# Hybrid window/banded attention with top-2 experts on one core: one rolling queue of rows per expert, expert outputs added straight into the output by accumulating transfers, and VectorE's evictions of them at the end of a step

## What is computed

```
x = x + window_attention(group_norm(x))     # 8x8 windows, shifted by 4, 8 heads, cosine scores, relative bias
t = t + banded_attention(layer_norm(t))     # blocks of 128 tokens, 4 heads, causal band of 32
t = t + experts(layer_norm(t))              # 8 experts, the 2 likeliest of each token, 128 -> 256 -> 128, exact gelu
    probs = softmax(xf @ gate_w + gate_b);  top2_vals, top2_idx = top_k(probs, 2)
    acc = acc + cw[:, e, None] * (gelu(xf @ W1[e] + b1[e]) @ W2[e] + b2[e])
```

## Time and profile before

| | us |
|---|---|
| median of 3 runs (2977.64 to 3004.55) | 2999.1 |
| the profiled execution | 2989.77 |
| its span, first to last instruction | 2988.0 |

### The profile page before, as it was taken

One profiled execution on the slowest core, in us unless ns is written; L12 is line 12 of the kernel. 1 busy time (PEld: TensorE's weight loads), 2 busy tenths in 40 slices (PEclk: granted clock), 3 DMA queues, 4 the chain that ended last, 5 costly groups with the idle time before them and its releaser, 6 DMA issues. The chain is left out here.

```text
span 2988.0 us, 75732 instructions
## 1 busy us (share of the span) xinstructions
PE 2511.1 (84%) x27338; PEld 1770.3 (59%) x27338; DVE 1996.7 (67%) x5193; ACT 1872.4 (63%) x3478; POOL 1670.3 (56%) x1626
## 2 busy tenths in 40 slices
PE   6888898888998889889989898888988787766673
PEld 3465555656666666666666666665666565544452
DVE  3678877887666666776766687777866676543223
ACT  3666666667667677677777677777766565443231
POOL 1224445554333444565555566777637888877765
PEclk9999999999999999899999899999999798977897
DMA  6233344335445554153443444554433333347674
GB/s 216 103 115 124 132 166 158 128 129 201 135 135 177 171 182 166 59 155 101 123 123 112 119 135 117 149 148 131 137 105 111 113 107 98 100 129 256 193 240 158
DMA packets 255504, 422.65 MB, mean 141 GB/s; under 512 B 42044, under 2 KB 141512, under 8 KB 252688
## 3 DMA queue, kind: packets, MB, share of 16 engines
q1 hardware_dynamic: 209632, 322.59, 33.5%
q0 software_dynamic: 35456, 72.95, 8.1%
q10 hardware_dynamic: 10048, 22.28, 2.4%
HBM read 205.05 MB, written 231.63 MB: 146 GB/s over the span
## 5 line engine op out<-in xcount | busy, mean ns | idle before, releaser
L1308 POOL DMA_INDIRECT x_sorted<-xn_c,place_i x512 | 537.1, 1049 | 333.5 <-PE bank_s L780 127.4
L1298 POOL TENSOR_TENSOR s_sb_a<-s_sb_a,mx_a 128x512 f32<-128x512 f32 x256 | 268.0, 1047 | 675.9 <-DVE mx_a L1703 675.0
L1329 POOL DMA_INDIRECT yg<-y_sorted,place_i x320 | 317.7, 993 | 187.9 <-PE bank_to L863 84.1
L1695 DVE TENSOR_TENSOR s_sb_a<-bank_s,bias_a 128x512 f32<-128x512 f32 x256 | 176.5, 690 | 327.1 <-PE bank_s L780 242.7
L1320 POOL DMA_INDIRECT y_tokens<-yo,back_to x276 | 284.9, 1032 | 93.8 <-issue 73.9
L909 PE MATMUL bank_m<-xe,wk_e 128*128 128x512 f32 x552 | 279.5, 632 | 47.6 <-ACT hid L1176 27.9
L917 PE MATMUL bank_m<-wk_e,hid 128*128 128x128 f32 x2208 | 288.0, 294 | 1.2 <-ACT hid L1176 1.2
L917 PEld LDWEIGHTS bank_m<-wk_e,hid 128*128 128x128 f32 x2208 | 282.5, 211 | 2.6 <-issue 1.9
L1298 POOL TENSOR_TENSOR s_sb_b<-s_sb_b,mx_b 128x512 f32<-128x512 f32 x256 | 269.9, 1054 | 0.3
L1142 ACT ACTIVATE p_sb_a<-s_sb_a 128x512 f32<-128x512 f32 x256 | 160.8, 628 | 161.0 <-POOL s_sb_a L1298 160.5
L841 PE MATMUL bank_to<-k_consts,p_sb_b 128*128 128x128 f32 x1024 | 178.5, 300 | 91.3 <-ACT pt_sb_a L1137 66.0
(11 more groups left out here) (233 smaller groups left out, 5947.0 us busy)
## 6 DMA issues: line engine op xcount, KB each, us to landing
y_sorted<-t_back SPq DMA_DIRECT2D x192, 512.0 KB, 5.2
wk_e<-in_w_experts_dram SPq DMA_DIRECT2D x134, 321.0 KB
xs<-x_sorted SPq DMA_DIRECT2D x134, 258.0 KB
y_sorted<-yo SPq DMA_DIRECT2D x101, 256.0 KB
t_kept<-t SPq DMA_DIRECT2D x64, 256.0 KB
xin<-in_x_dram SPq DMA_DIRECT2D x128, 112.0 KB
x_res<-in_x_dram SPq DMA_DIRECT2D x256, 56.0 KB
t_back<-t_kept SPq DMA_DIRECT2D x23, 512.0 KB
```

Source lines behind the costliest of these rows:

```text
L1298: pool.tensor_tensor(s[:, :, :], s[:, :, :], m[:, :, None].to_broadcast(shape), ALU.subtract).then_inc(s_sub[w], 1)
L1308: pool.indirect_dma_start(out=x_sorted[group_of[d] % XSIDES].ap(), out_offset=bass.IndirectOffsetOnAxis(ap=place_i[:, d % KEPT, TILES * ch ...
L1329: pool.indirect_dma_start(out=yg[:, c % 2, n, :], out_offset=None, in_=y_sorted[side].ap(), in_offset=bass.IndirectOffsetOnAxis(ap=place_i ...
L1695: tt(s_sb[0][:, :, :].rearrange("p (r h) n -> p r (h n)", h=2), scores, bias_a[:, kind, :, :].rearrange("p (r h) n -> p r (h n)", h=2), AL ...
```

## The change

**One queue for each expert, rolling over all images.** `GROUPS` is gone. `x_sorted` is one buffer with room for all images' rows in each expert's region. From image 1 on, each image is a batch: DVE's `tile_table` runs for every image, takes as many whole tiles of 512 rows as the queues hold (4 per image, 1 for image 1), and keeps in `start_row` how far each queue has been read. Only the last image takes the rounded-up rest (18 tiles), behind pads that SP writes once (`set_pads`). That makes 135 tiles in 68 pairs.

**Two slots in a pass.** Transposes in step 1 or 6, hidden layer in 2 or 7, outputs in 3 or the next 0. The first single tile is in pass 5, one pair in pass 6, two in each of passes 7 to 33, one in pass 34, and 11 pairs (22 tiles) in the tail. Fillers on PE end at pass 5 instead of 10. In the tail SP alone loads; two of its pairs are of image 30, nine of image 31.

**Output by accumulation.** The spill writes the residual straight into the output (eight transfers per half image instead of one); POOL then adds each tile's rows to it with four indirect transfers that accumulate in DRAM (540 in all). Before a tile's first one POOL waits until all of the tile before it has landed. `y_sorted`, its zero fill, `y_tokens`, the gathers, `t2_kept`, the way back, `sum_experts` and `store_image` are gone. The weight travels with the row as a 130th number (`SHARE`), which DVE writes three times per image (once for the first choice, twice for the second, after the first choice's scatters of that half have landed; before, images 20 to 31 alone had such writes, L1594).

**VectorE.** `slots_back` stands at the end of the step; it adds the bias in PSUM and then multiplies by the weight on the way to `yo`, two instructions for each tile instead of one.

```diff
-GROUPS = (7, 7, 6, 5, 4, 3)
+BATCH, FIRST_BATCH = TOP * TOKENS // SLOTS, 1
+MAX_TILES = TOP * IMAGES * TOKENS // SLOTS + E - 1
+FULL_TILES = 1 + BATCH * (IMAGES - 1 - FIRST_BATCH - 1)
+LAST_TILES = MAX_TILES - FULL_TILES
-SLOTS_PER_PASS = 3
+SLOTS_PER_PASS = 2
+BACK_AT = (((4, 0), (4, 1), (4, 2), (4, 3), (5, 1), (5, 2), (6, 1), (6, 2)),
+           ((9, 0), (9, 1), (9, 2), (9, 3), (10, 1), (10, 2), (10, 3), (11, 1)))
...
+            if i >= pairs[u].batch + (5 if n == 0 else 4) and not last:
                 here[n] = u
...
+        def landed(eng, done):
+            if done > 0:
+                k = (done - 1) % YO
+                eng.wait_ge(y_back[k], 16 * SUB * len(range(k, done, YO)))
...
             def spill(c, h):
                 need_half(sp, ln_c, c, h, LN_STEPS, 1)
-                sp.dma_start(t2_kept.ap()[c, :, HALF * h:HALF * h + HALF],
-                             t2[:, 4 * h:4 * h + 4, :].rearrange("p t d -> p (t d)")).then_inc(t2_out[h], 16)
...
+                        sp.dma_start(out_rolled[c, r, c0:c1, tiles, :],
+                                     t2[SIDE * r + p0:SIDE * r + p1, tiles, :]).then_inc(t2_out[h], 16)
...
+            def add_back(u, k):
+                _, q, _ = pairs[u].members[k // SUB]
+                j = k % SUB
+                if j == 0:
+                    for h in range(2):
+                        pool.wait_ge(t2_out[h], 16 * IO_DMAS * (pairs[u].batch + 1))
+                    if q == 0:
+                        pool.wait_ge(spare_set, 32)
+                    landed(pool, q)
+                    pool.wait_ge(ids_kept, q + 1)
                     pool.wait_ge(yo_ready, q + 1)
+                pool.indirect_dma_start(out=out,
                                         out_offset=bass.IndirectOffsetOnAxis(ap=back_to[:, q % IDS, j:j + 1], axis=0),
+                                        in_=yo[:, q % YO, j, :], in_offset=None, compute_op=ALU.add).then_inc(y_back[q % YO], 16)
...
+            def second_shares(d, h):
                 dve.wait_ge(scattered[h], 16 * (TILES * d + 4))
+                shares(d, 1, slice(4 * h, 4 * h + 4))
...
+            def slots_back(pair, banks):
+                for m, q, _ in pair.members:
+                    dve.wait_ge(y_done, q + 1)
+                    y = banks[:, m, :].rearrange("p (j d) -> p j d", j=SUB)
+                    bias = wk_b[buffer_of(q)[0]][:, None, B2_AT:B2_AT + D]
+                    tt(y, y, bias.to_broadcast([P, SUB, D]), ALU.add).then_inc(y_biased, 1)
+                for m, q, _ in pair.members:
+                    landed(dve, q - YO + 1)
+                    dve.wait_ge(y_biased, q + 1)
+                    y = banks[:, m, :].rearrange("p (j d) -> p j d", j=SUB)
+                    share = xs_b[buffer_of(q)[0]][:, :, SHARE:SHARE + 1]
+                    tt(yo[:, q % YO, :, :], y, share.to_broadcast([P, SUB, D]), ALU.mult).then_inc(yo_ready, 1)
...
-                if back is not None:
-                    for m, q, _ in back.members:
-                        slots_back(q, m, bank_m)
...
+                if back is not None:
+                    slots_back(back, bank_m)
```

591 lines of the change are left out of this document (186 added, 405 removed).

## The result

The changed kernel takes 3118.2 us (median of 4 runs, 3093.8 to 3122.1) against 2993.9 for the kernel before in the same comparison: a ratio of 1.040, 95% interval 1.033 to 1.048. Forecast were 2855 us and "faster" with 0.80. The profiled execution took 3118.9 us, its span is 3117.1.

A forecast was written before the change was run, and what follows sets the result against it. It took PE with its lockstep as the bound up to pass 28, then POOL's issue for the last 730 us. Pass 32 at 2509 us, last scatter 2671, last batch 2705, tail 135, end 2843; median forecast 2855, own range 2800 to 2910.

The forecast's parts named there:

- The pass: Passes 7 to 31, 25 of them with two pairs each: 81.0 us a pass, 2025 us in all.
- the base: Steady passes: the old kernel's two-pair passes 10 and 17, mean 80.1 us, taken as the starting price of a pass.
- the rival of 84 us: Steady passes get no shorter than three-pair passes: 84 us each, +75, near 2930 us; chance 0.30, alone or with dearer tail.
- the 0.9 us of table or clock: Part of the rival of 84 us: 0.9 us a pass from the table or clock, beside 2.5 us of scatter waits.
- VectorE's doubled eviction and its place: Steady passes: table and doubled evictions cost nothing to 5.0 us a pass; 0.9 taken, as VectorE idles for PE's outputs.
- POOL stops being last: Steady passes: transfers of 41 us and softmax of 17 us keep POOL busy for 58 of 81 us.
- To pass 7, passes 32 to 34: Start and late passes: pass 7 starts at 484 us, pass 32 at 2509, pass 34 at 2620; last scatter ends at 2671.
- Start of the last batch: After the last scatter: landing, pads, loads, transposes, gelus and evictions put the last batch's first add 34 us later, at 2705.
- The tail: Last 18 tiles: three transfers of 1.27 us, then the fourth until landed; 7.5 us a tile, 135 us (range 115 to 182).
- The rival "slower": Accumulating transfers hold POOL 1.9 us and land after 7: at least 5 us more per pass, near 3100 us; chance 0.12.
- break-even: In the rival "slower": from about 1.6 us of POOL work and 5.5 us to landing, the 145 us won are lost.
- An add as two reads: Accumulating transfers: two source reads halve the rate; moving time is hidden except each tile's fourth; tail grows by under 20 us.

The follow-up runs named there:

- e2: e1 with each tile's rows going to one of three scratch tensors and no wait for the landing of the tile before: 2981.8 us, ratio 0.997.
- e12: e9 with plain transfers into scratch tensors and no landing wait, except in the last three batches: 2726.3 us, ratio 0.913.
- e10: e9 with POOL's adds put behind the softmax subtraction of their step and the last ones a step later: 2820.1 us, ratio 0.945.
- e9: e4 with the first pair of each pass two steps later (steps 3 to 5) and POOL's adds starting two steps later: 3052.2 us, ratio 1.020.
- e7: The changed kernel without the second write of shares and POOL's waits for them: 3090.8 us, ratio 1.036.
- e6: The changed kernel with the table of tiles moved from VectorE's step 4 to the end of its step 7: 3114.5 us, ratio 1.041.
- e11: e10 with the table of tiles also moved from VectorE's step 4 to its step 7: 2831.1 us, ratio 0.948.
- e4: The changed kernel with VectorE's evictions back in the middle of its step instead of at its end: 3125.1 us, ratio 1.045.
- e1: The changed kernel with plain overwriting transfers to the output instead of adds, all waits kept: 3034.7 us, ratio 1.013.
- e3: The changed kernel with adds kept, but into one of three scratch tensors and without the landing wait: 3064.8 us, ratio 1.026.
- e17: e9 with every add in its step there, those ahead of the softmax subtraction put behind it: 3070.9 us, ratio 1.026.

## Why the prediction was wrong, step by step

**The pass (+172 us).** The failed step is the base: "the mean of passes 10 and 17, 80.1 us". Both had their two pairs at steps 3 to 7 and 0, and the change has the first at steps 1 to 3. I named this difference, under the rival of 84 us, and priced it at no more than the 0.9 us of table or clock. It was the main term: with POOL relieved the place is worth 12.1 us a pass (e2 against e12). With the pair in the base's place the base was too long for e10 (76.9 us) and too short for e9 (85.2), where the dear adds hold the pass. The means to see it were in the trace: cut the passes by steps rather than as a whole, and ask of each step what it takes without the pair. Pass 9 before, without expert work, takes 6.9 and 8.0 us in steps 2 and 3 and 11.3 and 9.1 in steps 4 and 5. That rival (0.30) came nearest in kind, but its 84 us fell short of 87.9 too. Of its two prices the wait for scatters is worth 1.2 us (e7), the table nothing (e6, e11).

**VectorE's doubled eviction and its place (+0.9 in my sum).** The place: right in this layout, e4 shows no difference. The doubling itself no run isolates.

**POOL stops being last (58 of 81 us).** Right for the changed kernel (e2: the same pass without the dear adds). With the pair in the base's place it is wrong (e12 against e9: 9.2 us a pass).

**To pass 7, passes 32 to 34 (+42 us).** Pass 5 and 6 were priced at 3.5 and 6.9 us a tile or pair, by the same base; the late steps at an estimate without the dear add. No run isolates the start. From pass 32 to the last scatter the change takes 198 us, and 178 without the add and the wait (e2), so the two cost 20 us of it.

**Start of the last batch (+19 us).** 33.5 us after the last scatter POOL adds again, as the forecast's 34 says, but it adds image 30. The step that failed is "POOL has 4 tiles of image 30 to fill 30 of these": only two were there, the other two came behind image 31's transposes on TensorE and then took 19.4 us on POOL ahead of the last batch. That 33.5 and 34 agree is luck: image 31's own first tile was evicted 40 us after the last scatter (2925.2) and added after 52.9.

**The tail (+41 us).** The form was right: four transfers, the fourth until it lands, then the next tile. Mis-sized were two terms. The add's POOL work, "0.96 us", measured 1.56 in the tail, so three transfers take 1.8 us more per tile. The fourth with its landing, chosen as 3.4 + 0.3 us, is 4.16 (median), 0.46 more. 18 x 2.25 us are the 41. e1, without the add, gives 2.9 us a tile back: its 6.9 lie below the 7.5 forecast, since a plain landing takes 3.07 and not 3.7.

**The rival "slower" (3100 us, 0.12).** Its time came nearly true, its mechanism only by half. POOL's work, 1.60 us, lay at its break-even, the landing (4.2 us, not 7) far below, and the 5 us per pass that it counted were zero: e2 and e3 leave the pass alone. It hit the number because the layout, which it didn't contain, cost as much.

**An add as two reads.** The Trainium skill (Collectives: The Full Stack, The bandwidth ceiling: the fold count and why AG ≠ RS ≠ AR) was read as a cost of moving. GpSimd's queue agrees in kind, first in the change, then in e1:

```profile
q0 software_dynamic: 94144, 69.54, 15.8%
```

```profile
q0 software_dynamic: 33664, 69.54, 7.1%
```

The same 69.54 MB, scatters included, cost the DMA engines more than twice the time with adds. Little of it reached the path: behind the end of POOL's work the landing came 0.5 us later, some 9 us in 18 tiles, and the prediction's estimate was under 20. POOL's own work, 0.6 us a transfer, weighed more.

## What to carry to other kernels

A base taken from a few stretches holds only for their layout: when a change moves work between the steps of a lockstep loop, price it per step, as what that step takes with the work less what it takes without, and look for the step in which TensorE already waits. There expert products were nearly free and the clock stayed up; two steps earlier the same products cost 12 us more a pass, with POOL relieved (e2 against e12). Second, with equal work, the steps in which the adds fall were worth 8 to 9 us a pass (e9 and e17 against e10). Count, for each step, the transfers and the waits for landings that stand ahead of what others need; which of the two did it here is open. Third, read a landing time from many places: the first one in e1, 4.12 us, would have said that an add lands no later, the other 16 say 1.1 us.
